# A post-norm decoder layer with top-1 experts on one core: three changes around the routing tail and the loads, and value moves issued by ScalarE

## The reference

```
x = layernorm(x + self_attention(x))             # 16 heads of 16, rotary on q and k, biases
x = layernorm(x + cross_attention(x, ctx, ctx))  # 16 heads of 64, causal and length mask, WO (1024, 256)
x = layernorm(x + experts(x))                    # 14 experts, 256 -> 512 -> 256
```

## Time and profile before

| | us |
|---|---|
| median of 3 runs | 537.02 (536.97 to 537.09) |
| the profiled execution | 539.74 |
| its span, first to last instruction | 538.0 |
| PE / PEld / DVE / ACT / POOL busy | 465.9 / 399.7 / 340.5 / 310.7 / 210.8 |
| mean granted TensorE clock | 0.935 |

### The profile page before, as it was taken

How to read it: one execution, slowest core, us unless ns; L and a number is a source line. 1 busy time by engine, 2 the same in 40 slices (tenths; PEclk the granted TensorE clock), 3 DMA queues, 4 the chain that set the end, 5 groups by cost and what they waited for, 6 DMA issues and landing times. The chain is left out here.

```text
span 538.0 us, 12482 instructions
## 1 busy us (share of the span) xinstructions
PE 465.9 (87%) x4364; PEld 399.7 (74%) x4364; DVE 340.5 (63%) x950; ACT 310.7 (58%) x1403; POOL 210.8 (39%) x294
## 2 busy tenths in 40 slices
PE   3504998999999999999999999999999772999991
PEld 2303776888787888888887888888888671999991
DVE  2733778587759667876678768864467534356553
ACT  2341676576877756876778757767476512343330
POOL 1412453443425454444335444632052412134443
PEclk9855899899999999999999999999999885899996
DMA  4771008463242510555051410600001973999200
GB/s 163 192 162 31 2 20 307 150 217 110 81 148 66 175 31 20 189 166 207 28 182 37 159 27 15 214 20 23 25 22 45 312 278 96 361 374 373 71 26 16
DMA packets 43033, 69.19 MB, mean 129 GB/s; under 512 B 12167, under 2 KB 33144, under 8 KB 42251
## 3 DMA queue, kind: packets, MB, share of 16 engines
q1 hardware_dynamic: 39574, 39.18, 23.4%
q10 hardware_dynamic: 926, 25.83, 13.7%
q0 software_dynamic: 2464, 3.31, 2.0%
HBM read 58.45 MB, written 29.77 MB: 164 GB/s over the span
## 5 line engine op out<-in xcount | busy, mean ns | idle before, releaser
L1025 ACT ACTIVATE probs<-bank,neg_max 100x100 f32<-100x100 f32 x512 | 169.8, 368 | 35.0 <-DVE neg_max L1151 26.3
L932 POOL TENSOR_TENSOR probs<-probs,row_inv 100x400 f32<-100x400 f32 x128 | 111.2, 888 | 129.1 <-DVE row_inv L1156 129.0
L1025 ACT ACTIVATION_READ_ACCUMULATOR probs<-bank,neg_max 100x1 f32 x512 | 118.1, 231 | 0.0
L1151 DVE TENSOR_REDUCE neg_max<-bank 100x4 f32<-100x400 f32 x128 | 67.7, 564 | 9.7 <-PE bank L1452 8.4
L1463 PE MATMUL bank<-ident,probs 100*100 100x100 f32 x512 | 68.3, 256 | 3.1 <-DVE probsT L1163 1.7
L1463 PEld LDWEIGHTS bank<-ident,probs 100*100 100x100 f32 x512 | 50.8, 130 | 15.8 <-issue 6.2
L1163 DVE COPY probsT<-bank 100x400 f32<-100x400 f32 x71 | 40.5, 571 | 22.7 <-PE bank L1463 21.8
L1378 PE MATMUL bank<-yT,W_Q 128*128 128x250 f32 (+1 forms) x224 | 50.7, 369 | 0.0
L1034 ACT COPY probsT<-bank 100x400 f32<-100x400 f32 x57 | 28.3, 496 | 37.1 <-PE bank L1463 33.6
L1304 PE MATMUL bank<-cT_h,W_K 128*128 128x250 f32 (+1 forms) x224 | 47.6, 297 | 1.5 <-DVE qk L1103 0.9
L1701 ACT ACTIVATE hT<-bank,b1c 128x128 f32<-128x128 f32 x72 | 20.5, 368 | 38.7 <-PE bank L1651 38.7
(11 more groups left out here) (159 smaller groups left out, 961.0 us busy)
## 6 DMA issues: line engine op xcount, KB each, us to landing
expert_rows<-c_empty ACTq DMA_DIRECT2D x13, 1935.0 KB, 8.8
w<-in_L_ffn_w_dram SPq DMA_DIRECT2D x36, 512.0 KB, 10.2
vX<-v_tile SPq DMA_DIRECT2D x14, 200.0 KB
vX<-v_tile SPq DMA_DIRECT2D x12, 150.0 KB
xs<-in_x_dram SPq DMA_DIRECT2D x12, 125.0 KB
vX<-v_tile SPq DMA_DIRECT2D x12, 100.0 KB
kX<-in_L_xattn_WK_dram SPq DMA_DIRECT2D x2, 512.0 KB, 7.2
qX<-in_L_xattn_WV_dram SPq DMA_DIRECT2D x2, 512.0 KB, 6.4
```

The costliest lines, as they stand in the source:

```text
L932: probs_ready.mark(pool.tensor_tensor(v, v, r, ALU.mult), step)
L1025: i = act.activation(probs[:, k % SLOTS, w], sc_bank[p % 2 * 2 + u][0:T, w], ACT.Exp, bias=neg_max[:, k % SLOTS, h:h + 1], accum_out=row_s ...
L1151: max_ready.mark(dve.tensor_reduce(neg_max[:, k % SLOTS, :], src, AX_X, ALU.max, negate=True), step)
```

## The change

1. **Logits ahead of the norm.** `rT` now transposes the sum before the second norm (`y1`) as soon as `added.x` is done. The mean over the row is taken out of the router weights once (`wr_sum` on TensorE, `wr_sum_out` on VectorE), so the logits of the unnormed rows differ from the true ones by the factor `rstd` alone. `top`, `choose`, `count`, `rank` and `place` need only their order; for the gate, `scale` multiplies by `rstd`, which is now kept for each tile (`rstd_x`).
2. **One-hot insertion.** The rows of tiles 10, 11 and 12 for the first blocks of experts 0 and 1 reach the experts block through TensorE. `hot` (VectorE) makes a matrix of zeros and ones out of `place_f`; `insert` multiplies the normed rows with it and adds the first 128 rows of the two experts as the table held them after tile 9, which SyncE loads into `xs` (`early_in`). The two transposed blocks stand in four PSUM banks when the attention block ends; ScalarE copies them, and TensorE does not transpose these two. The scatters of tiles 10 to 12 still run, for all other blocks, and wait for the early load. ScalarE loads the gelu table first. `xin` of expert 2 is loaded first, and blocks 2 and 3 are transposed behind `fc1` of block 1.
3. **New load order.** Piece 2 is loaded behind 5 and 6; context tiles 2 and 3 leave the list and are loaded behind piece 2 and behind pieces 7, 8; the routing constants, `v_bias` and the router weights are loaded behind context tile 5. `STEPS` is written anew: `K.0` and `V.0` stand ahead of the first `turn`, piece 2 is split later, and throughout the list some emptyings of banks change between ScalarE and VectorE (33 + 27 copies by ScalarE where it was 27 + 30, 17 `Q_out_a` for 23, 9 `V_out_a` for 13, 18 `K_out_a` for 13, 9 `rT_out_a` for 3).
4. **Moves.** The 50 moves stand in ScalarE's stream, at their places in the list, with the same waits.
5. Both blocks are opened with `no_gpsimd_drain=True`.

The diff, cut to its core (the list is shown by its last steps):

```diff
-added.x.11 copy_a.x.15.1.1 stats.x.11 id.11 pv.x.15.1 rstd.x.11 o_hi.x.15.1 ln.x.11 o_lo.x.15.1 rT.11
-wo.12 rT_out_a.11 logits.11 added.x.12 logits_out.11 id.12 stats.x.12 top.5 rstd.x.12 gate.5 choose.5 count.5
-ln.x.12 rank.5 place.5 rT.12 rT_out_a.12 logits.12 scatter.10 logits_out.12 top.6 gate.6 choose.6 count.6 scatter.11
-rank.6 place.6 scatter.12
+pv.x.15.1 rstd.x.11 logits.11 o_hi.x.15.1 ln.x.11 o_lo.x.15.1 logits_out.11 wo.12 top.5 scale.5 choose.5 count.5
+gate.5 rank.5 added.x.12 place.5 rT.12 id.12 rT_out_a.12 stats.x.12 logits.12 scatter.10 hot.5 scatter.11
+logits_out.12 insert.5 top.6 choose.6 count.6 rstd.x.12 scale.6 ln.x.12 gate.6 rank.6 place.6 scatter.12 hot.6
+insert.6
...
-            block = att.enter_context(nc.Block())
+            block = att.enter_context(nc.Block(no_gpsimd_drain=True))
...
-                load_piece(2)
                 for k in (3, 4):
                     load_piece(k)
...
                 for k in (5, 6):
                     load_piece(k)
+                load_piece(2)
+                load_c(2)
...
-                for k in (7, 8, 9, 10):
+                for k in (7, 8):
                     load_piece(k)
+                load_c(3)
+                for k in (9, 10):
+                    load_piece(k)
...
                         load_c(n)
-                    elif kind == "move":
-                        move(*step[1:])
+                        if n == 5:
+                            load_late()
...
+                for k in range(Y2S):
+                    wait(scattered[k], 16 * len(range(k, INSERT_FROM, Y2S)))
+                wait(*ln_done.at(("ln", "s", INSERT_FROM)))
+                for e in range(INSERTED):
+                    sp.dma_start(xs[:, 1 + e, :], rows[CAP * e:CAP * e + P, 0:D]).then_inc(early_in, 16)
...
             @block.scalar
...
+                def move(b, c, t):
+                    wait(*taken(("V", t, c)))
+                    if b >= 2:
+                        wait(*pv_done.at(("pv", "x", b - 2, c)))
+                    of_batch, of_tile = shared_rows(b, t)
+                    act.dma_start(vX[of_batch, b % 2, c * (DC // 2):(c + 1) * (DC // 2)], v_tile[of_tile, c, :]).then_inc(v_moved[2 * (b % 2) + c], 16)
...
+                    elif kind == "hot":
+                        wait(*took.at(("place", n)))
+                        wait(*projected.at(("qkT", NT - 1)))
+                        for t in pair_of_tiles(n):
+                            for e in range(INSERTED):
+                                i = dve.tensor_scalar(hot_of(t, e), iota[0:size(t), :], place_f[0:size(t), t:t + 1], float(-CAP * e), ALU.subtract, ALU.is_equal)
...
+                    elif kind == "insert":
...
+                        for e in range(INSERTED):
+                            for c in range(KC):
+                                across, to = slice(c * P, (c + 1) * P), sc_bank[INSERTED * c + e][:, 0:P]
+                                if n == INSERT_FROM // 2:
+                                    pe.matmul(to, xs[:, 1 + e, across], ident[:, :], start=True, stop=False, skip_group_check=True)
+                                for t in tiles:
+                                    i = pe.matmul(to, y2[0:size(t), t % Y2S, across], hot_of(t, e), start=False, stop=(t == NT - 1), skip_group_check=True)
...
-    X_LOADS = ((0, 1), (1, 2), (2, 4), (4, 8), (8, NE))
+    X_LOADS = ((2, 3), (0, 2), (3, 4), (4, 8), (8, NE))
...
+    def turned_after(n):
+        return [k for k in ({0: (), 1: (2, 3)}.get(n, (n + EARLY,))) if k < ALWAYS]
...
         def take_x(n):
-            act.wait_ge(xT_ready, n + 1)
+            if n < INSERTED:
+                act.copy(xTs[:, n % SLOTS_X, 0, :], xT_bank[n][:, 0:P])
+                act.copy(xTs[:, n % SLOTS_X, 1, :], h_bank[n][:, 0:P]).then_inc(xT_taken, 1)
+                return
+            act.wait_ge(xT_ready, n + 1 - INSERTED)
```

More of the change, by code:

```diff
@@ L44 @@
 Y2S = 4
+INSERTED = 2
+INSERT_FROM = 10
 OB = 2
@@ L152 @@
-max.s.9.0.1 qkT_out_a.8 max.s.9.1.0 exp.s.9.0.0 keys_p.10 ln.x.3 pv.s.8.1 V_out_v.4.1 exp.s.9.0.1 rT.3 max.s.9.1.1
-move.5.1.4 move.6.1.4 v.10 rT_out_v.3 turn.x.5.0.0 o_hi.s.8.1 v_out.10 logits.3 exp.s.9.1.0 inv.s.9.0 o_lo.s.8.1
-Q.2.2 norm.s.9.0.0 copy_v.x.5.0.0 logits_out.3 norm.s.9.0.1 top.1 gate.1 choose.1 count.1 out.6 Q_out_a.2.2
-turn.x.5.0.1 added.s.6 copy_a.x.5.0.1 rank.1 stats.s.6 exp.s.9.1.1 Q.2.3 place.1 rstd.s.6 ln.s.6 turn.s.9.0.0
-scatter.2 Q_out_a.2.3 cT.6 copy_v.s.9.0.0 scores.s.10.0 x_load.10 c_load.8 cT_hi.6 inv.s.9.1 turn.s.9.0.1 cT_lo.6
@@ new lines @@
+o_lo.x.2.1 turn.x.3.0.1 max.x.4.1.0 wo.1 exp.x.4.0.1 copy_v.x.3.0.1 mask.5 max.x.4.1.1 inv.x.4.0 norm.x.4.0.0
+norm.x.4.0.1 turn.x.3.1.0 added.x.1 K.2.1 exp.x.4.1.0 copy_v.x.3.1.0 id.1 stats.x.1 rT.1 K_out_a.2.1 turn.x.3.1.1
+rstd.x.1 rT_out_v.1 pv.x.3.0 copy_v.x.3.1.1 exp.x.4.1.1 ln.x.1 logits.1 move.5.0.4 K.2.2 logits_out.1 o_hi.x.3.0
+inv.x.4.1 top.0 norm.x.4.1.0 scale.0 o_lo.x.3.0 gate.0 out.5 norm.x.4.1.1 K_out_v.2.2 pv.x.3.1 added.s.5 choose.0
+count.0 scores.s.8.0 o_hi.x.3.1 turn.x.4.0.0 max.s.8.0.0 rank.0 copy_a.x.4.0.0 o_lo.x.3.1 K.2.3 exp.s.8.0.0 place.0
@@ new lines @@
+qkT_out_a.11 pv.x.8.0 rT_out_a.5 keys_v.13 keys_p.14 turn.x.8.1.1 o_hi.x.8.0 logits.5 copy_a.x.8.1.1 o_lo.x.8.0
+K.4.3 rstd.x.5 logits_out.5 top.2 ln.x.5 pv.x.8.1 scale.2 K_out_a.4.3 choose.2 count.2 out.9 gate.2 o_hi.x.8.1
+scores.s.13.0 added.s.9 o_lo.x.8.1 rank.2 max.s.13.0.0 wo.6 place.2 exp.s.13.0.0 max.s.13.0.1 scatter.4 max.s.13.1.0
+exp.s.13.0.1 stats.s.9 scatter.5 V.8.0 max.s.13.1.1 exp.s.13.1.0 inv.s.13.0 added.x.6 norm.s.13.0.0 stats.x.6 rT.6
+exp.s.13.1.1 scores.x.9.0 id.6 rT_out_v.6 rstd.s.9 V_out_v.8.0 norm.s.13.0.1 turn.s.13.0.0 inv.s.13.1 max.x.9.0.0
@@ new lines @@
+copy_a.x.10.0.1 max.s.15.0.1 V.9.1 exp.s.15.0.0 max.s.15.1.0 rstd.x.7 logits_out.7 max.s.15.1.1 turn.x.10.1.0 ln.x.7
+exp.s.15.0.1 cT.11 pv.x.10.0 copy_v.x.10.1.0 V_out_v.9.1 cT_hi.11 turn.x.10.1.1 move.12.0.9 inv.s.15.0 o_hi.x.10.0
+top.3 out.11 move.11.1.9 cT_lo.11 norm.s.15.0.0 copy_a.x.10.1.1 scale.3 exp.s.15.1.0 o_lo.x.10.0 K.5.0 norm.s.15.0.1
+added.s.11 choose.3 count.3 gate.3 pv.x.10.1 K_out_a.5.0 stats.s.11 rank.3 move.12.1.9 exp.s.15.1.1 turn.s.15.0.0
+place.3 K.5.1 rstd.s.11 copy_v.s.15.0.0 o_hi.x.10.1 scatter.6 inv.s.15.1 ln.s.11 turn.s.15.0.1 K_out_a.5.1 K.5.2
```

432 lines of the change are left out of this document (228 added, 204 removed).

## The result

Time after: 534.08 us median of 6 runs (532.29 to 535.74), beside 537.06 for the kernel before (6 runs, 536.64 to 538.7). The ratio is 0.9925, 95% interval 0.9906 to 0.9945: faster by 0.55 to 0.94%. The forecast was 520.0 with a range of 511 to 532, so the time lies above the range. The profiled execution took 532.4, its span is 530.5.

The account below looks back on a forecast made before the run. TensorE was taken to bound the middle (60 to 420 us) and the experts. Profiled 539.7 - 16.5 (start) - 5.4 (tail) + 5 (moves) = 522.8; runs' median lies 2.7 lower: 520.1, stated as 520, range 511 to 532.

Parts of the forecast that it names:

- The start: Before 60 us: context tile 2 loaded about 20 us earlier, first `turn` at 38 instead of 55.4; gain 16.5 us.
- The clock: Granted clock in the early stretch, 0.5 when idle and 0.56 behind it; nothing counted for it.
- The load order: SyncE's early loads: `v_bias` loads, 5.2 us, no longer delay context tile 2; nothing counted for their new place.
- The tail: Routing's end, last `added` to first `fc1`: earlier `place_i`, then no drain of 3.54 us; gain 5.4 us, bounds 1.9 and 6.8.
- Weights spreading out: Before 442 us: without moves in SyncE's list the expert-weight transfers no longer leave together at 417; nothing counted.
- Moves on ScalarE: Middle, 60 to 420 us: 50 move issues of 0.762 us on ScalarE delay TensorE; cost 5 us, between 0 and 38.
- rival (a): Moves on ScalarE cost nothing or less than 1 us; 515 to 516 us, chance 0.2.
- rival (b): Moves on ScalarE cost 10 to 20 us because delays add up; 525 to 535 us, chance 0.17.
- For the others the wait empties the queue too: Moves whose `V_out` ScalarE does not do itself: their wait also empties its queue; worst case 38 us of ScalarE delay.
- so an issue costs nothing when work is already queued: ScalarE's stream: an issue at 87.22 us ran ahead of a queued cast without a gap, so such issues are free.
- The new list as a whole: Order of steps in the middle, where TensorE idled 8.3 us: taken as 0, with -3 to +3 us.
- More than 20 us of idle time in the middle shows (b): Sign: TensorE's idle time from 60 us to attention's last 20 us, expected about 13; above 20 means move delays add up.

Follow-up runs that it names:

- SE: Changed kernel with the 50 moves issued by SyncE again and `v_bias` loaded early, behind the last weight piece: 516.9 us, ratio 0.9597 to the kernel before.

## Why the prediction was wrong

**The start, right.** 18.4 us in place of 16.5, first `turn` at 37.3 for 38, idle time 17.3 in 15 to 20, no wait of TensorE for a context load. The clock, for which the prediction counted nothing, is 0.97 before 60 us in the profiled execution; in the kernel before it was 0.72.

**The load order, wrong: the step that failed most.** The prediction moved the `v_bias` loads out of context tile 2's way, counted only what this frees, and so put their new place at nothing. It did not ask who reads `v_bias`: `vb_hi.0` does, in the middle of the first batches, and the loads now leave behind context tile 5. The loss is 9.0 us, of which the trace places 7.8: a wait of 5.8, and behind it 6 us at a clock of 0.65. Of a step that is moved, ask also what it is moved behind.

**The tail, half right.** 4.3 in place of 5.4. The second half came as written: from the end of `place_i` to `fc1` 4.1 us, forecast 4.4, before 8.5. The first half gave nothing: up to `place_i` 8.2 us, forecast 6.7, before 8.0. `rank.6` behind `insert.5` was named ("Twelve matmuls of `insert.5` (2.4 us) lie before `rank.6`") but taken to be hidden, and VectorE waited 1.04 us for it. That `gate.6` reads `rstd` ahead of `place.6`, for another 1.28, was not seen. So taking the logits from unnormed rows gained nothing on this way, with the list as it is.

**Weights spreading out, wrong: "I count nothing for it".** The prediction saw that SyncE without moves would issue the weights earlier, and valued it only as relief for the early load. They met the last moves instead, and a move's landing is what `V_out` waits for. Loss 3.8 us, the balance of 7.4 lost at 390 us and 3.7 gained in the tail, where the weights and the early load are out of the way sooner.

**Moves on ScalarE, right in size, in kind only in part.** 5 predicted, 5.7 to 6.1 measured in three pairs, each uncertain by about 2. They are not free (rival (a)) and don't cost 10 to 20 (rival (b)). The working put all 5 into idle time of TensorE in the middle, up from 8.3 to about 13. Measured with the moves in the one or the other stream, and the weights held back in both, that idle time (60 to 420 us) goes from 10.7 to 12.5 in one pair and from 11.0 to 12.5 in another. What the moves delay by waits is the 2.7 us of the markers, where two moves stand together, and this is the loss that the prediction described ("A pair of moves is 1.5 us"), at about half its size. That the total came near 5 is in part luck: the rest of it that the traces place is a lower clock, which the prediction did not have.

"For the others the wait empties the queue too" and "so an issue costs nothing when work is already queued" fit both runs with 0.45 us, but don't say where it turns. The Trainium skill, "Advanced Engine Details and Errata", section "Engine Queue Depths", gives ScalarE a queue of 8. By that rule eight entries would be four heads of `exp` here (an activation and a read of its sum each, 0.34 us a head), an estimate of 1.4 us of cover. The trace agrees roughly: without a wait, two issues in a row (1.06 us) cost a stretch 0.2 us at most, and every stretch that loses 0.4 to 1.3 us has four or more in a row, 2.4 us at least; one with five in a row loses nothing. The prediction's own reading of this rule was loose: the issue at 87.22 ran ahead of four instructions that stood before it, not of eight.

**The sum.** 520.0 - 1.9 (start) + 1.1 (tail) + 0.9 (moves) + 9.0 (`v_bias`) + 3.8 (weights) = 532.9; 1.2 us up to the measured 534.1 are within the uncertainty. The new list as a whole, which the prediction put at 0 with -3 to +3, may be in them: in SE, without any of the three losses, TensorE's idle time from 60 to 420 us is 10.7 us, before the change 8.3.

**The check that misled.** "More than 20 us of idle time in the middle shows (b)": it was 22.1, and (b) was false. 10.9 of them are two single waits (5.79 and 5.08), for causes that the list of rivals did not have. A total can't tell many small losses from two large ones; the waits of TensorE by line can.

## What to carry to other kernels

When transfers leave a queue or change place in it, two lists are needed: what leaves earlier and what that will meet, and what leaves later and who reads it. A transfer on a compute engine costs little while the issues that follow each other are short beside the work queued there, and steeply more beyond: look for places where several stand together. A wait in front makes it worse, 16.8 us in place of 8.9 here. A fixed cost such as a drain is worth removing only together with what waits behind it: 0 alone, 3.4 us with the insertion. And a result that is ready earlier gains nothing while the instruction in front of its reader still waits for something else, as `gate.6` did ahead of `place.6`.

## What the runs showed of the hardware

The length of an issue does not follow its bytes: 50 issues of 100 x 2 KB from on-chip memory to DRAM took 0.28 us each, 64 x 512 bytes 0.45, and the moves (up to 100 x 2 KB within on-chip memory) 0.78. A second one right behind another takes 0.61 in place of 0.45. The eight strided `v_bias` loads held SyncE for 5 us at 40 us and for 9 us at 64 us. A move of 200 KB was not complete 8 us after its issue beside eight weight transfers of 512 KB; with these held back, VectorE's wait for it fell from 6.2 to 1.3 us.

Between the statistics at 95 and at 129 us the same work took 33.4 us in the kernel with moves on SyncE (SE, mean clock 0.95 in that stretch) and 31.8 in that with the issues alone (1.00): 1.6 us that go with the granted clock, of the order of the spread of each kernel's runs.
